# Stationary-weight projection of q and k with pieces placed by transfers, and transposed row maxima placed from one copy

## The chip, the cores and the metric

The kernel runs on one core of one Trainium2 chip. The metric is the device time of one launch in microseconds (us). TensorE is written PE, its weight loads PEld, VectorE DVE, ScalarE ACT, GpSimd POOL; SP (SyncE) computes nothing here and issues the transfers (DMAs).

## The reference

Eight batch elements of 512 positions and 256 features go through a layer norm, sliding-window attention with 32 query heads on 8 key/value heads, and a gate: silu of a projection of the 8-bit rounded input.

```
xn = layernorm(x)
q = xn @ Wq + bq; k = xn @ Wk + bk; v = xn @ Wv + bv     # 32, 8, 8 heads of 64
q, k = interleaved_rope(q, cos, sin) * SCALE, interleaved_rope(k, cos, sin) * SCALE
#   first = even * cos - odd * sin;  second = odd * cos + even * sin
scores = q k^T, masked to |i - j| <= 128; one sink logit per head joins the softmax
s = (softmax(scores with sink) without sink @ v) @ Wo + bo
x = x + s * silu(fp8(xn) @ W.T + b)
```

Products are kept near full float32 by splitting an operand into a rounded high part and a low remainder (names ending in hi/high and lo/low) and multiplying the parts.

## The kernel before

The work is 64 steps, one for each batch element (8) and key/value head (8, with its group of 4 query heads), and each step has 4 tiles q of 128 positions. The engines run their own programs and meet through semaphores. The order within a tile is written out by hand; each step works on three stages at once: it projects tile q of step it+2, turns and takes row maxima of step it+1, and does scores, exponentials, the weighted sum and the output projection of step it (the weighted sum one tile late, the transposition of its result two, the output projection three). Loops (Fori) run over batch elements and pairs of groups; two steps before the first are written apart and fill the pipeline while x is normalised and the weights are split.

In a tile, `project` (L974) multiplies the tile of x (stationary) with 384 columns of weights: 4 query heads, one key head and one value head. `projected` (DVE, L760) adds the bias; `turn` (POOL, L431 to L438) applies the rotation; `split_hi` (ACT) and `split_lo` (POOL, L444) make the parts side by side in `qk_parts`. TensorE then transposes them against an identity: `turn_q_full` (L983) each tile, `turn_k` (L995) once a step, and ACT copies the results (L534, L538). `score_rows` (L1016) gives scores by rows for the maxima (`maximum`, DVE L772), `negated` makes `neg_parts`, `turn_max` (L1001) transposes them, and ACT places the rows by 4 copies with a mask (L552) into partitions 64 to 71 of `qT_high`. So `scores` (L1028 and L1030, two matmuls for each block of 128 keys) gives scores with the maximum already taken off, `exps` (ACT L529) exponentiates them, `cut` (POOL L464) clears the corners, `weigh` (L1042) sums values, `turn_o` (L1051) transposes, and `out_project` (L1063) accumulates over the groups. The chunks `turn_x`, `turn_xq` and `ffn` stand in some tiles of steps 1, 6 and 7 of a batch element.

The wait that decides the order at a score is

```
at(pe, s_exp_done, NB, c + 1, blk - 1)
```

that is, with two score banks, a third block waits for the exponential of the first. In a tile of before, the projection and the turns stand between the second and the third block.

## Time and profile before

| | |
|---|---|
| time, median of 3 runs | 1935.78 us (1932.91 to 1942.27) |
| the profiled execution | span 1928.5 us from its first to its last instruction; the profile gives no device time of its own beside it |
| PE busy | 1818.4 us (94%) |
| DVE, ACT, POOL busy | 71%, 73%, 61% |
| mean granted TensorE clock | 0.983 |
| transfers | 20672 packets in SP's queue, 25.45 MB, 4.0% of 16 engines |

Times are us from the start of the span. In a line of a timeline the first number is the start and the second the duration; x6 means six instructions merged. In a group of the page the numbers after the bar are the busy time in us, the mean of one in ns, and the idle time of the engine just before them. In a line of windows stand the stretch, its length, the busy time of PE, PEld, DVE, ACT and POOL with the number of instructions, the granted clock of TensorE as a share of 2.4 GHz, the busy share of the DMA engines and GB/s. "issue" in the chain is time in which an engine waited for nothing that the profile shows.

### The profile page before, as it was taken

The numbers are of one execution on the slowest core, as the hardware profiler recorded it, in microseconds if no ns is written. First come the engines' busy times: TensorE is split into PE (matmuls) and PEld (weight loads), VectorE is DVE, ScalarE is ACT, GpSimd is POOL, SyncE is SP. The second block draws the span as 40 slices with busy tenths as digits, with TensorE's granted clock in tenths as the row PEclk, the third lists the DMA queues.
The fourth block names the chain that finished last, engine by engine and source line by source line (L and its number), as shares of the span: only waits on it lengthen the run. The fifth ranks groups of instructions, "written<-read, shape, count | busy, mean of one in ns | idle before, by whom it ended". The sixth has DMA issues, their size and how long they took to land.

```text
span 1928.5 us, 48655 instructions
## 1 busy us (share of the span) xinstructions
PE 1818.4 (94%) x13199; PEld 1707.6 (89%) x13199; DVE 1373.2 (71%) x4883; ACT 1406.3 (73%) x3764; POOL 1183.6 (61%) x1511
## 2 busy tenths in 40 slices
PE   3499999999999999999999999999999999999997
PEld 2399998999989999899989999899998999889996
DVE  8776776777767777767767777577777676776775
ACT  3277777777767777777867777677877787777775
POOL 4465656666566666666656666566666665665654
PEclk9699999999999999999999999899999999999999
DMA  5200000000000000000000000000000000000000
GB/s 191 82 8 2 0 1 25 12 2 0 13 20 5 1 0 18 19 2 0 1 19 18 2 0 1 30 7 2 0 18 19 2 1 1 18 24 2 0 1 17
DMA packets 20889, 28.07 MB, mean 15 GB/s; under 512 B 1344, under 2 KB 19264, under 8 KB 20544
## 3 DMA queue, kind: packets, MB, share of 16 engines
q1 hardware_dynamic: 20672, 25.45, 4.0%
q8 instruction: 103, 1.69, 0.4%
q14 instruction: 114, 0.93, 0.2%
HBM read 21.25 MB, written 4.19 MB: 13 GB/s over the span
## 4 chain that ended last, share of the span: by engine, by line
PE 86%; DVE 5%; issue 4%; ACT 1%; DMA 0%; DVEq 0%; POOLq 0%; POOL 0%; ACTq 0%
PE pv_bank L1042 26%; PE ring L974 15%; PE ring L1016 10%; PE acc L1063 9%; PE score L1028 8%; PE score L1030 7%; PE ring L983 5%; PE ring L1051 3%; PE ring L995 2%; PE ring L964 1%; PE ring L1001 1%; DVE junk L772 1%; DVE neg_max L781 1%; DVE sink_arg L786 1%; DVE proj L760 1%
## 5 line engine op out<-in xcount | busy, mean ns | idle before, releaser
L1042 PEld LDWEIGHTS pv_bank<-v,stage 128*128 128x128 f32 x5136 | 682.5, 192 | 4.7 <-issue 1.1
L1042 PE MATMUL pv_bank<-v,stage 128*128 128x65 f32 x5136 | 674.0, 266 | 0.9 <-DVE o_norm L800 0.9
L772 DVE CUSTOM_DVE_ANT_0 junk<-ring,mask 128x384 bf16<-128x384 f32 (+1 forms) x1036 | 507.0, 490 | 224.9 <-PE ring L1016 198.3
L529 ACT ACTIVATE stage<-score 128x512 f32<-128x512 f32 x640 | 357.0, 588 | 283.1 <-PE score L1030 282.3
L464 POOL TENSOR_SCALAR_AFFINE_SELECT stage<-stage 128x512 f32<-128x512 f32 x384 | 243.2, 641 | 425.1 <-ACT stage L529 425.1
L1016 PE MATMUL ring<-kT_high,qT_full 128*128 128x384 f32 (+1 forms) x1036 | 398.9, 385 | 16.6 <-DVE proj L760 15.4
L444 POOL TENSOR_TENSOR qk_parts<-turned,qk_parts 128x320 fp32r<-128x320 f32 x263 | 227.3, 864 | 207.0 <-ACT qk_parts L564 207.0
L552 ACT ACTIVATE qT_high<-ring,own_rows 8x128 fp32r<-8x128 f32 x1032 | 284.9, 345 | 13.7 <-PE ring L1001 7.3
L1028 PE MATMUL score<-qT_full,kT_high 128*128 128x512 f32 x640 | 267.7, 418 | 16.1 <-issue 14.9
L760 DVE TENSOR_TENSOR proj<-ring,bias 128x384 f32<-128x384 f32 x264 | 145.7, 552 | 183.7 <-PE ring L974 183.2
L1030 PE MATMUL score<-qT_high,kT_low 72*128 72x512 f32 x640 | 256.3, 400 | 0.0
L1016 PEld LDWEIGHTS ring<-kT_high,qT_full 128*128 128x128 f32 x1036 | 199.8, 193 | 50.3 <-DVE proj L760 15.8
L438 POOL TENSOR_TENSOR turned<-turned,turn_s 128x320 f32<-128x320 f32 x264 | 229.6, 870 | 20.7
L431 POOL TENSOR_TENSOR turned<-proj,cos 128x320 f32<-128x320 f32 x264 | 228.8, 867 | 21.9 <-DVE proj L760 21.9
L434 POOL TENSOR_TENSOR turn_s<-proj,sin 128x320 f32<-128x320 f32 x264 | 229.8, 870 | 0.0
L974 PE MATMUL ring<-w_hi,xT_hi 128*128 128x384 f32 (+1 forms) x528 | 197.0, 373 | 27.3 <-DVE proj L760 17.5
L534 ACT ACTIVATE qT_full<-ring 128x512 fp32r<-128x512 f32 x259 | 155.6, 601 | 43.3 <-PE ring L983 43.1
L974 PE MATMUL ring<-w_hi,xT_lo 128*128 128x384 f32 (+1 forms) x528 | 182.5, 346 | 0.0
L974 PE MATMUL ring<-w_lo,xT_hi 128*128 128x384 f32 (+1 forms) x528 | 182.0, 345 | 0.0
L983 PEld LDWEIGHTS ring<-ident_r,qk_parts 128*128 128x128 f32 x1036 | 156.4, 194 | 21.5 <-DVE inv_scale L821 0.3
L538 ACT ACTIVATE qT_high<-qT_full 64x512 fp32r<-64x512 f32 x259 | 163.3, 631 | 6.4
L1063 PE MATMUL acc<-wo_hi,oT_hi 128*128 128x256 f32 (+1 forms) x518 | 156.6, 302 | 0.4 <-DVE oT_lo L806 0.4
(110 smaller groups left out, 3282.4 us busy)
## 6 DMA issues: line engine op xcount, KB each, us to landing
x_in<-in_x SPq DMA_DIRECT2D x13, 512.0 KB, 3.6
x_res<-in_x SPq DMA_DIRECT2D x18, 256.0 KB, 3.3
out<-x_res SPq DMA_DIRECT2D x16, 256.0 KB, 2.2
stage<-in_w_qkv SPq DMA_DIRECT2D x4, 768.0 KB, 5.0
gate<-in_x SPq DMA_DIRECT2D x4, 512.0 KB, 4.1
stage<-in_w_o SPq DMA_DIRECT2D x4, 512.0 KB, 3.6
bias<-in_b_qkv SPq DMA_DIRECT2D x1, 1152.0 KB, 6.6
bias<-in_b_qkv SPq DMA_DIRECT2D x1, 384.0 KB, 7.8
```

What stands on the lines that cost most here:

```text
L434: nc.gpsimd.tensor_tensor(turn_s[:, :].rearrange("p (h i t) -> p h i t", i=D // 2, t=2), x_qk.rearrange("p (h i t) -> p h i t", i=D // 2, ...
L464: nc.gpsimd.affine_select(out=pr, in_=pr, compare_op=ALU.is_ge, fill=0.0, base=0, pattern=[[0, GROUP], [sign, P]], channel_multiplier=-sign) \
L529: nc.scalar.activation(prob[:, q % 2 * 3 + n, :], score[(FIRST[q] + n) % 2][:, :], ACT.Exp) \
L552: last = nc.scalar.activation(qT_high[D:D + NR, q, h * P:(h + 1) * P], ring[2][0:NR, 0:P], ACT.Copy, scale=own_rows[:, h:h + 1])
L772: nc.vector.tensor_tensor_reduce(junk[:, h % 2, 0:cols], ring[h % 2][:, 0:cols], mask[:, m0:m0 + cols], 1.0, LOWEST, ALU.add, ALU.max, row ...
L974: last = nc.tensor.matmul(ring[1][:, 0:PW], left[:, k, q * P:(q + 1) * P], of_group(right[:, k, :], g, PW), start=(n == 0), stop=(n == len ...
L983: last = nc.tensor.matmul(ring[0][:, h * P:(h + 1) * P], qk_parts[:, par, q, h * HW:h * HW + 2 * D], ident_r[:, :], start=True, stop=True)
L1016: nc.tensor.matmul(ring[h % 2][:, 0:cols], qT_full[:, q, h * P:(h + 1) * P], kT_high[:, par, k0 * P:k0 * P + cols], start=True, stop=True) ...
L1028: nc.tensor.matmul(score[blk % 2][:, :], kT_high[:, par, k * P:(k + 1) * P], qT_full[:, q, :], start=True, stop=False)
L1030: nc.tensor.matmul(score[blk % 2][:, :], kT_low[0:D + NR, par, k * P:(k + 1) * P], qT_high[0:D + NR, q, :], start=False, stop=True).then_i ...
L1042: last = nc.tensor.matmul(pv[:, h, :], prob[:, q % 2 * 3 + n, h * P:(h + 1) * P], v[:, par, k, :], start=(n == 0), stop=(n == len(BLOCKS[q ...
L1063: last = nc.tensor.matmul(acc[q // 2][:, (q % 2) * M:(q % 2 + 1) * M], left[:, q % 2, k * P:(k + 1) * P], w_g, start=fresh and k == 0 and ...
```

## The change

The weights become the stationary operand for q and k. The even and the odd elements of the four query heads of a group are 128 columns each, so `project` (now 128 weight columns against all 512 positions, six matmuls) gives them transposed already: `queries(a, 0)` and `queries(a, 1)` at the start of each step, for step a = it+2. Keys come for four groups at once (`QUAD`), twice a batch element, and values for all eight groups by tile, four times a batch element; `chunk_at` puts these into the tiles (1, 2), (1, 3), (5, 2), (5, 3) for keys and (7, 1), (7, 2), (7, 3) and (0, 1) of the next for values, as (group, tile). Bias and copy of q are on ACT (`even_out`, `odd_out`), the rotation and the low parts on POOL (`turn_even` to `second_low`), bias and rotation of k on DVE (`keys_turn`).

A group's pieces then lie 32 partitions to a head, and the scores need 64 in a row for each head, with a high part below. SP places them by transfers from SBUF to SBUF of 32 partitions by 512 elements (64 KB): `queries_in` twice, 12 transfers each, and `keys_in`, 6 transfers, every step. The row maxima are turned for two tiles at once, copied once by ACT, and placed by `rows_in`, 4 transfers of 2 partitions, twice a step. All loops are written out (no Fori), the normalised x stays in its input buffer, 8 instead of 9 elements are normalised ahead, and the first 8-bit rounding moves into step 0.

```diff
-            def turn(a, q):
...
-                    .broadcast_to([P, GROUP + 1, D // 2, 2])
-                nc.gpsimd.tensor_tensor(turned[:, slot, :].rearrange("p (h d) -> p h d", d=D),
-                                        x_qk.rearrange("p (h d) -> p h d", d=D), cos_q, ALU.mult) \
-                    .then_inc(s_turn_self, 1)
-                nc.gpsimd.tensor_tensor(turn_s[:, :].rearrange("p (h i t) -> p h i t", i=D // 2, t=2),
-                                        x_qk.rearrange("p (h i t) -> p h i t", i=D // 2, t=2)[:, :, :, ::-1],
-                                        sin_q, ALU.mult).then_inc(s_turn_self, 1)
-                at(pool, s_turn_self, 2 * TILES, a, 2 * q + 2)
-                nc.gpsimd.tensor_tensor(turned[:, slot, :], turned[:, slot, :], turn_s[:, :], ALU.add) \
-                    .then_inc(s_turned_done, 1)
-
-            def split_lo(a, q, par):
-                at(pool, s_hi_done, 2 * TILES, a, 2 * q + 2)
-                parts = qk_parts[:, par, q, 0:(GROUP + 1) * HW].rearrange("p (h w) -> p h w", w=HW)
-                nc.gpsimd.tensor_tensor(parts[:, :, 0:D], turned[:, q % 2, :].rearrange("p (h d) -> p h d", d=D),
...
+            def turn_even(a):
+
+                pool.wait_ge(s_even_done, a + 1)
+                upto(pool, s_qT_first_in, Q_IN * a)
+                upto(pool, s_qT_second_in, Q_IN * a)
+                nc.gpsimd.tensor_tensor(q_first[:, :], q_even[:, :], cos[:, :], ALU.mult).then_inc(s_rope, 1)
+                nc.gpsimd.tensor_tensor(q_second[:, :], q_even[:, :], sin[:, :], ALU.mult).then_inc(s_rope, 1)
+
+            def turn_odd(a):
+
+                pool.wait_ge(s_odd_done, a + 1)
+                nc.gpsimd.tensor_tensor(q_second_hi[:, :], q_odd[:, :], sin[:, :], ALU.mult).then_inc(s_rope, 1)
+                pool.wait_ge(s_rope, 6 * a + 3)
+                nc.gpsimd.tensor_tensor(q_first[:, :], q_first[:, :], q_second_hi[:, :], ALU.subtract) \
+                    .then_inc(s_rope, 1)
+
+            def turn_rest(a):
+
+                nc.gpsimd.tensor_tensor(q_odd[:, :], q_odd[:, :], cos[:, :], ALU.mult).then_inc(s_rope, 1)
+                pool.wait_ge(s_rope, 6 * a + 5)
+                nc.gpsimd.tensor_tensor(q_second[:, :], q_second[:, :], q_odd[:, :], ALU.add).then_inc(s_rope, 1)
+
+            def first_low(a):
+                pool.wait_ge(s_first_hi, a + 1)
+                nc.gpsimd.tensor_tensor(q_first[:, :], q_first[:, :], q_first_hi[:, :], ALU.subtract) \
+                    .then_inc(s_first_lo, 1)
+
+            def second_low(a):
+                pool.wait_ge(s_second_hi, a + 1)
+                nc.gpsimd.tensor_tensor(q_second[:, :], q_second[:, :], q_second_hi[:, :], ALU.subtract) \
+                    .then_inc(s_second_lo, 1)
...
+            def keys_in(t):
+
+                quad, r = t // QUAD, slice(t % QUAD * HALF, (t % QUAD + 1) * HALF)
+                sp.wait_ge(s_k_lo, 2 * quad + 2)
+                upto(sp, s_score_pe, NB * (t - 2))
+                upto(sp, s_kT_in, K_IN * t)
+                for row, part in ((0, k_first_hi), (HALF, k_second_hi), (D, k_first_hi), (D + HALF, k_second_hi)):
+                    sp.dma_start(kT_high[row:row + HALF, t % 3, :].bitcast(F32), part[r, :]).then_inc(s_kT_in, 16)
+                for row, part in ((0, k_first), (HALF, k_second)):
+                    sp.dma_start(kT_low[row:row + HALF, t % 3, :].bitcast(F32), part[r, :]).then_inc(s_kT_in, 16)
+
+            def queries_in(a, row, low, high, ready, done):
+
+                sp.wait_ge(ready, a + 1)
+                upto(sp, s_score_pe, NB * (a - 1))
+                upto(sp, done, Q_IN * a)
+                for h in range(GROUP):
+                    r = slice(h * HALF, (h + 1) * HALF)
+                    sp.dma_start(qT_full[row:row + HALF, a % 2, h, :].bitcast(F32), low[r, :]).then_inc(done, 16)
+                    sp.dma_start(qT_full[D + row:D + row + HALF, a % 2, h, :].bitcast(F32), high[r, :]) \
+                        .then_inc(done, 16)
+                    sp.dma_start(qT_high[row:row + HALF, a % 2, h, :].bitcast(F32), high[r, :]).then_inc(done, 16)
+
+            def rows_in(s, pair):
+
+                sp.wait_ge(s_max_rows_done, 2 * s + pair + 1)
+                if s == 0 and pair == 0:
+                    sp.wait_ge(s_ones_ready, 3)
+                for h in range(GROUP):
+                    sp.dma_start(qT_high[D + 2 * h:D + 2 * h + 2, s % 2, h, pair * 2 * P:(pair + 1) * 2 * P]
+                                 .bitcast(F32), turned_rows[2 * h:2 * h + 2, :]).then_inc(s_rows_in, 16)
+
+            def result(n, j):
+
+                sp.wait_ge(s_fin_done, n * 2 + j + 1)
+                sp.dma_start(out_t[n][:, 2 * j:2 * j + 2, :], x_res[:, 2 * j:2 * j + 2, :]).then_inc(s_out_put, 16)
+
+            def step(it):
+                n, k = it // KV, it % KV
+                t, a = it + 2, it + 2
+                if real(t) and t % QUAD:
+                    keys_in(t)
+                if real(it):
+                    rows_in(it, 1)
+                if k == 0 and n >= 1:
+                    result(n - 1, 0)
+                if real(it + 1):
+                    rows_in(it + 1, 0)
+                if real(t) and t % QUAD == 0:
+                    keys_in(t)
+                if real(a):
+                    queries_in(a, 0, q_first, q_first_hi, s_first_lo, s_qT_first_in)
+                    queries_in(a, HALF, q_second, q_second_hi, s_second_lo, s_qT_second_in)
+                if k == 0 and n >= 1:
+                    result(n - 1, 1)
...
+            def even_out(a):
+                act.wait_ge(s_q_pe, 2 * a + 1)
+                upto(act, s_rope, 6 * (a - 1) + 2)
+                nc.scalar.activation(q_even[:, :], ring[1][:, :], ACT.Identity,
+                                     bias=q_bias[:, a % KV * 2:a % KV * 2 + 1]).then_inc(s_even_done, 1)
...
+            def max_rows(s, pair):
+
+                act.wait_ge(s_max_turned_pe, 2 * s + pair + 1)
+                upto(act, s_rows_in, 16 * GROUP * (2 * s + pair))
+                nc.scalar.activation(turned_rows[:, :].bitcast(F32R), ring[2][0:NR, 0:2 * P], ACT.Copy) \
+                    .then_inc(s_max_rows_done, 1)
...
+            def project(col, done):
+
+                products = [(w, xs, k) for k in range(KT)
+                            for w, xs in ((w_hi, xT_hi), (w_lo, xT_hi), (w_hi, xT_lo))]
+                for n, (w, xs, k) in enumerate(products):
+                    last = nc.tensor.matmul(ring[1][:, :], w[:, k, col:col + P], xs[:, k, :], start=(n == 0),
                                             stop=(n == len(products) - 1))
-                last.then_inc(s_proj_pe, 1)
-
...
+            def queries(a, odd):
+
+                if odd:
+                    pe.wait_ge(s_even_done, a + 1)
+                else:
+                    upto(pe, s_max_done, TILES * GROUP * (a - 1) if a > 1 else 0)
+                    if a == KV * 0:
+                        pe.wait_ge(s_k_turned, 4)
+                    if a == 1:
+                        pe.wait_ge(s_odd_done, 1)
+                    if a == 2:
+                        pe.wait_ge(s_w_lo_done, N_CHUNKS)
+                project(W_Q + (a % KV * 2 + odd) * P, s_q_pe)
+
+            def turn_max(s, pair):
+                pe.wait_ge(s_neg_done, 2 * s + pair + 1)
+                upto(pe, s_max_rows_done, 2 * s + pair)
+                for t in range(2):
+                    last = nc.tensor.matmul(ring[2][0:NR, t * P:(t + 1) * P], neg_parts[:, pair, t, :], ident_r[:, :],
+                                            start=True, stop=True)
+                last.then_inc(s_max_turned_pe, 1)
+
+            def score_rows(b, q, h, it):
+
+                if q == 0 and h == 0:
+                    pe.wait_ge(s_qT_first_in, Q_IN * (b + 1))
+                    pe.wait_ge(s_qT_second_in, Q_IN * (b + 1))
+                    pe.wait_ge(s_kT_in, K_IN * (b + 1))
+                if h == 1:
+                    other = chunk_at(it // KV, it % KV, q)
+                    if q == 0 and real(it + 2):
+                        pe.wait_ge(s_odd_done, it + 3)
+                    elif other is not None:
+                        ring1_read(other)
+                upto(pe, s_max_done, TILES * GROUP * b + GROUP * q + h - 1)
+                k0, cols = window(q)
+                nc.tensor.matmul(ring[h % 2][:, 0:cols], qT_full[:, b % 2, h, q * P:(q + 1) * P],
+                                 kT_high[:, b % 3, k0 * P:k0 * P + cols], start=True, stop=True).then_inc(s_max_pe, 1)
```

**PE, start of a tile.** Before, tile 0 of a step: from the second pair of score matmuls over the transposition of the query parts (`L983`) to the projection (`L974`).

```order
L1028 MATMUL score<-qT_full,kT_high 128x512 [waits exp_done]
L1030 MATMUL score<-qT_high,kT_low 128x512
L91 REGISTER_ALU
L91 ISA [waits lo_done]
L983 MATMUL ring<-ident_r,qk_parts 128x128 [waits max_done]
L983 MATMUL ring<-ident_r,qk_parts 128x128 x3
L91 ISA
L974 MATMUL ring<-w_hi,xT_hi 128x384 [waits max_done]
L974 MATMUL ring<-w_lo,xT_hi 128x384
L974 MATMUL ring<-w_hi,xT_lo 128x384
L974 MATMUL ring<-w_hi,xT_hi 128x384
L974 MATMUL ring<-w_lo,xT_hi 128x384
```

The same place now, from the first pair of score matmuls to the first row of scores for the maxima (`L1086`); `L1107` and `L1109` are the score pairs, `L1037` the projection of the odd elements of the queries.

```order
L1107 MATMUL score<-qT_full,kT_high 128x512 [waits exp_done,rows_in]
L1109 MATMUL score<-qT_high,kT_low 128x512
L1107 MATMUL score<-qT_full,kT_high 128x512 [waits exp_done]
L1109 MATMUL score<-qT_high,kT_low 128x512
L1037 MATMUL ring<-xT_hi,w_hi 128x512 [waits even_done]
L1037 MATMUL ring<-xT_hi,w_lo 128x512
L1037 MATMUL ring<-xT_lo,w_hi 128x512
L1037 MATMUL ring<-xT_hi,w_hi 128x512
L1037 MATMUL ring<-xT_hi,w_lo 128x512
L1037 MATMUL ring<-xT_lo,w_hi 128x512
L1086 MATMUL ring<-kT_high,qT_full 128x256 [waits kT_in,max_done,qT_second_in,qT_first_in]
L1123 MATMUL pv_bank<-v,stage 128x65 [waits cut_done,norm_done,exp_done,v_done]
```

The transpositions are gone, the projection has become six wide matmuls (six more, for the even elements, stand ahead of these rows), and the first row of scores now waits for the transfers (`qT_first_in`, `qT_second_in`, `kT_in`).

**SP, one step.** Before, the loop over batch elements, which holds four transfers for results in eight steps:

```order
L356 DMA x_res<-in_x 128x2x256
L357 ISA
L359 DMA out<-x_res 128x2x256 [waits fin_done]
L360 ISA
L356 ISA [waits out_put]
L356 DMA x_res<-in_x 128x2x256
L357 REGISTER_ALU
L359 DMA out<-x_res 128x2x256 [waits fin_done]
```

Now a part of one step: the last two transfers of `keys_in`, the two calls of `rows_in`, and the beginning of `queries_in`.

```order
L365 DMA kT_low<-k_first 32x512
L365 DMA kT_low<-k_second 32x512
L385 DMA qT_high<-turned_rows 2x256 [waits max_rows_done]
L385 DMA qT_high<-turned_rows 2x256 x3
L385 DMA qT_high<-turned_rows 2x256 [waits max_rows_done]
L385 DMA qT_high<-turned_rows 2x256 x3
L374 DMA qT_full<-q_first 32x512 [waits qT_first_in,score_pe,first_lo]
L375 DMA qT_full<-q_first_hi 32x512
L377 DMA qT_high<-q_first_hi 32x512
L374 DMA qT_full<-q_first 32x512
L375 DMA qT_full<-q_first_hi 32x512
L377 DMA qT_high<-q_first_hi 32x512
```

Each step has 38 such transfers in one queue; the first of a `queries_in` waits for the low part, for all score matmuls of step it (`score_pe`), whose buffer it overwrites, and the other 11 follow without a wait.

## Rows read from the trace of the kernel before

**Rows 1.** The page, part 4: the chain that ended last, by engine.

```profile
PE 86%; DVE 5%; issue 4%; ACT 1%; DMA 0%; DVEq 0%; POOLq 0%; POOL 0%; ACTq 0%
```

**Rows 2.** Windows of one batch element and of one plain step.

```profile
756.26:981.56 225.30, 220.24 (x1634) 207.92 (x1633) 161.51 (x587) 171.97 (x464) 142.44 (x181) 1.00 0.03 8
842.41:869.25 26.84, 26.84 (x203) 25.61 (x202) 19.31 (x72) 20.88 (x57) 17.28 (x23) 1.00 0.01 2
```

**Rows 3.** Timeline of TensorE in plain steps, start and duration in us.

```profile
902.14 0.56 PE L983 MATMUL ring<-ident_r,qk_parts 128*128 128x128 f32 x4
902.54 0.39 PE L974 MATMUL ring<-w_hi,xT_hi 128*128 x1
...
903.63 0.40 PE L1028 MATMUL score<-qT_full,kT_high 128*128 128x512 f32 x1
...
904.39 0.78 PE L1042 MATMUL pv_bank<-v,stage 128*128 128x65 f32 x6
904.98 0.42 PE L1016 MATMUL ring<-kT_high,qT_full 128*128 128x384 f32 x1
...
907.68 0.36 PE L1063 MATMUL acc<-wo_hi,oT_hi 128*128 x1
...
908.47 0.40 PE L1028 MATMUL score<-qT_full,kT_high 128*128 128x512 f32 x1
...
909.42 0.56 PE L983 MATMUL ring<-ident_r,qk_parts 128*128 128x128 f32 x4
...
919.47 0.36 PE L1016 MATMUL ring<-kT_high,qT_full 128*128 128x256 f32 x1
919.67 0.38 PE L1051 MATMUL ring<-ident,o_norm 128*128 128x128 f32 x2
919.89 0.56 PE L1042 MATMUL pv_bank<-v,stage 128*128 128x65 f32 x4
```

**Rows 4.** Groups by line and shape on ScalarE and GpSimd.

```profile
L529 ACT ACTIVATE stage<-score 128x512 f32<-128x512 f32 x640 | 357.0, 588 | 283.1 <-PE score L1030 282.3
L464 POOL TENSOR_SCALAR_AFFINE_SELECT stage<-stage 128x512 f32<-128x512 f32 x384 | 243.2, 641 | 425.1 <-ACT stage L529 425.1
L451 POOL TENSOR_TENSOR x_res<-x_res,gate 128x512 f32<-128x512 f32 x18 | 22.9, 1272 | 20.4 <-DVE gate L753 15.2 <-DMA x_res<-in_x 5.2
```

**Rows 5.** Timeline of the queue engine SP: its DMA issues.

```profile
19.95 0.33 SPq L333 DMA_DIRECT2D stage<-in_w_ffn  x1
20.32 0.43 SPq L328 DMA_DIRECT2D x_in<-in_x  x1
...
65.14 0.37 SPq L328 DMA_DIRECT2D x_in<-in_x  x1
65.55 0.51 SPq L350 DMA_DIRECT2D bias<-in_b_qkv  x1
```

**Rows 6.** The page, part 6: one issue group, KB each, median us to landing.

```profile
out<-x_res SPq DMA_DIRECT2D x16, 256.0 KB, 2.2
```

**Rows 7.** The chain in order of time: two of its seven long "issue" pieces.

```profile
321.27 1.98 issue
...
546.61 2.39 issue
```

**Rows 8.** Windows of 8 us after waits of TensorE, clock column in view.

```profile
96.00:104.00 8.00, 8.00 (x45) 7.49 (x46) 3.28 (x13) 4.77 (x13) 3.86 (x5) 0.73 0.07 24
544.00:552.00 8.00, 5.61 (x36) 5.10 (x35) 3.37 (x14) 3.23 (x8) 2.53 (x4) 0.93 0.03 9
552.00:560.00 8.00, 8.00 (x43) 7.76 (x42) 4.58 (x19) 3.54 (x11) 3.97 (x5) 0.64 0.00 0
1232.00:1240.00 8.00, 8.00 (x36) 7.80 (x35) 2.46 (x9) 4.28 (x12) 4.04 (x5) 0.50 0.00 1
```

**Rows 9.** Timeline of TensorE: the first scores, and the last weighted sum.

```profile
95.95 0.79 PE L1028 MATMUL score<-qT_full,kT_high 128*128 128x512 f32 x1 [1.19 <-ACT xqT L513]
...
1913.02 1.97 PE L1042 MATMUL pv_bank<-v,stage 128*128 128x65 f32 x16 [0.88 <-DVE o_norm L800]
```

More of the change, by code:

```diff
@@ L889, in step @@
[L889 to L896 removed]
+                        if real(b):
+                            maximum(b, q, h)
@@ L928, in _ @@
[L928 to L934 removed]
+            dve.wait_ge(s_x_odd_got, 16)
+            statistics(gate, range(TILES))
+            moments_of(1)
+            keys_turn(0, 0)
+            keys_turn(0, 1)
+            normalise(1, gate, range(TILES))
+            measure(1)
```

1214 lines of the change are left out of this document (558 added, 656 removed).

## Prediction

> **What bounds the kernel now.** The chain that ended last comes first: 86% of the span is TensorE's work [rows 1], so TensorE's time per step is the time. The windows come next: a plain step (842.41 to 869.25) takes 26.84 us with PE busy throughout, a batch element of eight steps 225.30 us at full clock [rows 2]. Eight plain steps are 214.7; the other 10.6 us are `turn_x`, `turn_xq`, `ffn` and one idle piece of about 2 us at a loop head, which comes back under the clock. The timeline then gives prices by distance from start to start, since matmuls overlap: six of the projection 902.54 to 903.63, 1.09 us; four of `L983` .40; two score pairs 908.47 to 909.42, .95, so .237 for a matmul of 512 columns; six of `weigh` .59; six of `out_project` .79; a row of 256 columns .20, `turn_o` .22 [rows 3]. The other engines have slack; a score block costs ACT 588 ns, and a float32 operation of 128x512 costs POOL 1272 ns [rows 4].
>
> **What TensorE saves.** Removed from a step: 4 times 1.09 of projection, 4 times .40 of `turn_q_full`, and the eight of `turn_k`, which I put at .75 (four like `L983`, four only 64 wide): 6.7. Left are 20.1 us. Added: 12 matmuls for the queries, 2.85; for keys 12 in four steps, .71; for values 24 in eight, .71 (four `turn_max` stay four). That is 24.4. Of the 10.6 us a batch element the loop piece of 2.0 goes with the loops, leaving 1.1 a step. A new wait appears: in tiles 1 and 2 the third score block has nothing ahead of it. Two pairs take .95, but the bank is free only after .47 + .59 of ACT and some .2 of hand-over: .35 lost, twice a step, less where a chunk stands between; I take .5. TensorE alone would need 26.0 a step where it needs 28.2.
>
> POOL does not stop it: eight operations of 1.27, 1.3 for keys and six `cut` of .64 make 15.3 us a step, counted from when the buffers come free; its last low part is ready after 8 times 1.27 and five cuts, 13.4 us. DVE loses `projected` and half of `negated`, ACT 16 small copies and five large ones; both were under 75%.
>
> **What SP adds.** This term decides. Follow the cycle from R, where TensorE takes the first row of tile 0 in step it. In step it, `queries_in` may start only when all scores of the step are done, the first half of tile 3 (`score_pe`), because it overwrites the buffer that they read. Then 24 transfers go out one behind the other, and the first row of step it+1 waits for the last to land. TensorE works meanwhile on what lies outside the cycle: the rest of tile 3 (rows .8, `weigh` 4 times .59, turn and output 1.0), then 2.85 of queries and .95 of scores: 8.0, with chunks in tile 3 .6 more on average, 8.6. Inside lie 26.0 - 8.6 = 17.4 us.
>
> An issue: SP's rows show .33 and .37 where nothing precedes, with a gap of .04, and .43 and .51 where the transfer follows directly on another [rows 5]. So the pitch lies between .37 and .55. These had 128 partitions, the new ones 32; I take .43, nearer the short end. 23 pitches are 9.9. Landing: 256 KB from SBUF took 2.2 us [rows 6]; a quarter of that I put at 1.9. With .2 for the two waits the queue part is 12.0. The step becomes 17.4 + 12.0 = 29.4, and TensorE stands idle for 12.0 - 8.6 = 3.4 us, 4.0 in a plain step, at one place. Behind that row queue `weigh` and both `turn_max`; POOL's `turn_even` waits for the same landing, and behind it its `cut`, which is needed five us later. `keys_in` (6) and `rows_in` (8) go out before or after the 24, where SP has time.
>
> **The clock.** Seven waits of about 2 us stand in the chain at loop heads, as pieces "issue", 1.98 to 2.39 [rows 7]. After the one at 546.61 the granted clock fell from its high level, 2.4 GHz, to the low one, 1.2: .93 and then .64 in windows of 8 us, 3.4 us lost by (1 - clock) times 8. From 1232 to 1240 it was .50 throughout, 4.0 us lost in that window alone; after the wait for which scores begin at 96, .73, 2.2 us [rows 8]. Not every such wait costs something: the batch element from 756.26 holds one and has 1.00 [rows 2]. A wait of 3.4 to 4 us in every step is longer than any of these, so I expect a fall in nearly every step; I take 2.4 us, near the lowest, since packed work follows. The Trainium skill ("TensorE: Matmul & The Clock Gate", section "HAM oscillation — how this bites in real kernels") describes this pattern, matmul groups parted by waits for transfers that restart at the low clock each time. It speaks against the change: by it every step pays, by the rows of waits of 2 us only some, and the sum would be 29.4 without the fall and 31.8 with it. The rows are of shorter waits, so the lengths, not the page, carry my choice.
>
> **Sum.** Before, scores began at 96 us, and 15.5 us remained from the last weighted sum [rows 9]. I put the new fill at 88 (one element fewer to normalise and no rounding ahead, about 15, against some 7 that x loads now queue behind 30 transfers), the end at 16 again. The last two steps have no queries to fetch and the last no rows: 23 + 17.5. So 88 + 62 times 31.8 + 40.5 + 16 = 2116 us of span. The profiled span was 1928.5, the median of runs 1935.8; with these 7 more, about 2120.
>
> **Rivals.**
> - *TensorE keeps the path; faster.* If the queue part takes under 8.6 us, SP is hidden. With landing and waits at 2.1 this needs a pitch below .28, or a landing much shorter; no row shows so little, but none shows 32 partitions out of SBUF. Then 144.5 + 62 times 26.0 + 7 = about 1765, up to 1830. For it speaks that .33 is itself an issue to another place.
> - *Queue-bound, but the clock holds.* At .37, the isolated pitch, the queue part is 10.6, the step 28.0, the idle 2.0 us, as long as waits of which some cost nothing: 1890. With a fall in every second step 1965. It crosses the time of before at about 28.7 us a step.
> - *The transfers themselves are slow.* If SP's pitch is .52, as where one followed another at once, the step is 33.9 and the time 2255; if each of the 64 KB transfers takes .6 us because 32 partitions share few ways in, 35.7 and 2365. Against it: in two of the windows the DMA share is .00 and in none above .07 [rows 8], so nothing else is in the way.
>
> The Trainium skill ("SBUF — State Buffer", the section on DMA port swizzle) gives 189 GB/s for 32 partitions at 1 MiB. By an estimate from that page 64 KB take .35 us, less than an issue, so by it SP and not the ways into SBUF sets the pace; no run here shows it.
>
> **How the numbers follow.** Queue-bound with the clock falling .55 (2000 to 2250 by pitches of .38 to .52), TensorE-bound .13, queue-bound with clock mostly held .20, transfers slower still .12. About 0.5% is what a measurement of this kernel can tell from no change. Faster takes the second case and most of the lower part of the third: .26. Same .04. Slower .70. The range leaves out most of the fast case and half of the slowest: 1840 to 2290. With cases on both sides, the likeliest one's own range is 2000 to 2250.
>
> **What would show it.** In the new profile: PE idle before `L1086` for 3 to 4 us in each of 62 steps, put down to a transfer into `qT_full` or `qT_high`; SP issues of .37 to .50 from start to start, 24 in a row; the chain with SP or DMA above 25% of the span and PE near 60%; a mean granted clock under .95; PE busy share down to about 80%; small waits of .35 us at `L1107` in tiles 1 and 2; 128x512 operations on POOL at 1.27. Wrong would be: `L1086` without a wait (then the pitch or the landing was mis-sized and the first rival holds), a clock of .98 or more with the wait in place (then the second), or a landing of over 3 us while SP is done (the third). If POOL's `L497` comes later than the scores of tile 3, the rotation is the gate and not the queue.

## The result and the profile after

The changed kernel takes 2535.86 us (median of 4 runs, 2534.69 to 2544.95), the kernel before 1937.19 in the same comparison (1932.91 to 1942.27): a ratio of 1.313, 95% interval 1.308 to 1.319. It is slower, as forecast and by the mechanism forecast, but the time lies far outside the range of 1840 to 2290. The page of the changed kernel, its spans, busy times and chain, answers to [rows 1], where PE had 86%:

```profile
span 2533.0 us, 35309 instructions
PE 1891.3 (75%) x11139; PEld 1675.2 (66%) x11139; DVE 1187.7 (47%) x4157; ACT 720.9 (28%) x1509; POOL 1008.5 (40%) x1019
...
q1 hardware_dynamic: 113296, 149.84, 22.8%
...
PE 52%; issue 19%; SPq 12%; DVE 3%; ACT 3%; POOL 3%; DMA 3%; POOLq 0%; DVEq 0%
```

No engine is over 75%: a cycle of waits sets the time, not an amount of work. Its waits (engine, line, releaser: total us, times, longest):

```profile
POOL q_first L473 <- DMA qT_high<-q_second_hi: 958.5, 62, 23.5
...
PE ring L1086 <- issue: 508.2, 63, 13.8
```

TensorE stands 8 us in each step before the first row of tile 0. SP's timeline of one step (start, duration), which answers to [rows 5], begins with the 24 transfers:

```profile
1202.39 0.54 SPq L374 DMA_DIRECT2D qT_full<-q_first  x1
1202.97 0.59 SPq L375 DMA_DIRECT2D qT_full<-q_first_hi  x1
1203.61 0.58 SPq L377 DMA_DIRECT2D qT_high<-q_first_hi  x1
1204.23 0.59 SPq L374 DMA_DIRECT2D qT_full<-q_first  x1
...
1216.26 0.59 SPq L375 DMA_DIRECT2D qT_full<-q_second_hi  x1
1216.90 0.59 SPq L377 DMA_DIRECT2D qT_high<-q_second_hi  x1
...
1241.77 0.54 SPq L374 DMA_DIRECT2D qT_full<-q_first  x1
```

TensorE's timeline has the row that waits for them:

```profile
1218.96 0.55 PE L1086 MATMUL ring<-kT_high,qT_full 128*128 128x256 f32 x1 [8.35 <-issue]
```

From these rows the cycle can be taken apart: 24 issues from 1202.39 to 1217.49 (15.1 us, .63 from start to start), 1.5 from the end of the last issue to the row, 22.8 until the next queries may start: 39.4 us. Read in the same way over the 62 steps, the mean is 15.4 + 1.5 + 21.1 = 38.0 us. In 47 of them the next queries start .07 us after the last score matmul. In the other 15, every fourth step, `keys_in` stands directly ahead of the queries, and SP is still issuing keys: it starts the queries 2.9 to 5.0 us after the scores, 50.1 us in all. The longest of these, where the last score ends at 214.45:

```profile
214.05 0.40 PE L1109 MATMUL score<-qT_high,kT_low 72*128 72x512 f32 x1
```

```profile
218.79 0.59 SPq L365 DMA_DIRECT2D kT_low<-k_second  x1
219.49 0.52 SPq L374 DMA_DIRECT2D qT_full<-q_first  x1
```

The clock, in windows of the step from 1202.39 (the number behind the busy times is the granted clock):

```profile
1210.00:1214.00 4.00, 0.61 (x3) 0.18 (x1) 0.00 (x0) 0.69 (x1) 0.00 (x0) 1.00 0.43 109
1214.00:1218.96 4.96, 0.00 (x0) 0.03 (x1) 0.00 (x0) 0.00 (x0) 0.00 (x0) 0.57 0.41 103
1218.96:1223.00 4.04, 4.04 (x20) 4.04 (x21) 0.96 (x5) 0.47 (x2) 3.96 (x4) 0.50 0.36 89
1223.00:1227.00 4.00, 4.00 (x17) 3.51 (x17) 2.73 (x9) 0.98 (x2) 1.63 (x2) 0.50 0.01 4
1227.00:1231.00 4.00, 3.63 (x24) 3.40 (x22) 2.07 (x5) 2.28 (x4) 3.56 (x4) 0.83 0.01 2
1231.00:1235.00 4.00, 4.00 (x27) 3.62 (x27) 3.39 (x15) 2.23 (x5) 2.08 (x3) 1.00 0.00 0
```

The clock falls to its low level, 1.2 GHz, inside the wait, and the next 8 us and more of packed work run at that level.

### The profile page after: what moved, and what is told of

Its sections match the earlier page's. It is cut to its first block, busy times and chain, and to the rows that moved or that the text cites. A ratio compares the mean times of both kernels' runs of the same rounds, so it can differ in the third digit from the quotient of the medians.

```text
span 2533.0 us, 35309 instructions
## 1 busy us (share of the span) xinstructions
PE 1891.3 (75%) x11139; PEld 1675.2 (66%) x11139; DVE 1187.7 (47%) x4157; ACT 720.9 (28%) x1509; POOL 1008.5 (40%) x1019
## 3 DMA queue, kind: packets, MB, share of 16 engines
q1 hardware_dynamic: 113296, 149.84, 22.8%
## 4 chain that ended last, share of the span: by engine, by line
PE 52%; issue 19%; SPq 12%; DVE 3%; ACT 3%; POOL 3%; DMA 3%; POOLq 0%; DVEq 0%
PE pv_bank L1123 18%; PE ring L1086 8%; PE acc L1146 7%; PE score L1107 5%; PE ring L1037 5%; PE score L1109 4%; SPq L375 4%; SPq L374 4%; DMA qT_high<-q_first_hi 3%; SPq L377 3%; PE ring L1133 2%; ACT stage L611 2%; PE ring L1046 2%; SPq L363 1%; POOL q_second L497 1%
## 5 line engine op out<-in xcount | busy, mean ns | idle before, releaser
L1086 PE MATMUL ring<-kT_high,qT_full 128*128 128x384 f32 (+1 forms) x1024 | 435.2, 426 | 574.3 <-issue 508.2
L1086 PEld LDWEIGHTS ring<-kT_high,qT_full 128*128 128x128 f32 x1024 | 229.9, 225 | 620.0 <-issue 555.3
L1107 PE MATMUL score<-qT_full,kT_high 128*128 128x512 f32 x640 | 283.0, 442 | 13.3 <-ACT stage L611 13.1
L1109 PE MATMUL score<-qT_high,kT_low 72*128 72x512 f32 x640 | 271.0, 423 | 0.0
L1107 PEld LDWEIGHTS score<-qT_full,kT_high 128*128 128x128 f32 x640 | 136.0, 213 | 66.3 <-ACT stage L611 48.4
L1037 PE MATMUL ring<-xT_hi,w_hi 128*128 128x512 f32 x320 | 145.8, 456 | 27.2 <-ACT q_even L617 18.9
L1146 PE MATMUL acc<-wo_hi,oT_hi 128*128 128x256 f32 x512 | 162.3, 317 | 0.6 <-DVE oT_lo L885 0.6
L1146 PE MATMUL acc<-wo_lo,oT_hi 128*128 128x256 f32 x512 | 161.5, 316 | 0.0
L1146 PE MATMUL acc<-wo_hi,oT_lo 128*128 128x256 f32 x512 | 160.8, 314 | 0.0
L1109 PEld LDWEIGHTS score<-qT_high,kT_low 72*128 72x128 f32 x640 | 134.4, 210 | 17.9
L1037 PE MATMUL ring<-xT_hi,w_lo 128*128 128x512 f32 x320 | 131.9, 412 | 0.0
L1037 PE MATMUL ring<-xT_lo,w_hi 128*128 128x512 f32 x320 | 131.4, 411 | 0.0
L885 DVE TENSOR_TENSOR oT_lo<-ring,oT_hi 128x256 fp32r<-128x256 f32 x256 | 108.6, 424 | 34.6 <-ACT oT_hi L652 31.5
L1146 PEld LDWEIGHTS acc<-wo_hi,oT_hi 128*128 128x128 f32 x512 | 116.4, 227 | 0.8 <-DVE oT_lo L885 0.8
```

The lines of the kernel that those rows point to most:

```text
L885: nc.vector.tensor_tensor(oT_lo[:, q % 2, :], ring[2][:, 0:KT * P], oT_hi[:, q % 2, :].bitcast(F32), ALU.subtract).then_inc(s_oT_lo_done, 1)
L1037: last = nc.tensor.matmul(ring[1][:, :], w[:, k, col:col + P], xs[:, k, :], start=(n == 0), stop=(n == len(products) - 1))
L1086: nc.tensor.matmul(ring[h % 2][:, 0:cols], qT_full[:, b % 2, h, q * P:(q + 1) * P], kT_high[:, b % 3, k0 * P:k0 * P + cols], start=True, s ...
L1107: nc.tensor.matmul(score[blk % 2][:, :], kT_high[:, c % 3, k * P:(k + 1) * P], qT_full[:, c % 2, :, q * P:(q + 1) * P], start=True, stop=F ...
L1109: nc.tensor.matmul(score[blk % 2][:, :], kT_low[0:D + NR, c % 3, k * P:(k + 1) * P], qT_high[0:D + NR, c % 2, :, q * P:(q + 1) * P], start ...
L1146: last = nc.tensor.matmul(acc[q // 2][:, (q % 2) * M:(q % 2 + 1) * M], left[:, q % 2, k * P:(k + 1) * P], right[:, col:col + M], start=fre ...
```

## The experiments

**Theory**: SP's issues and what lands behind them set the step, and the clock adds to it. Rivals: the bytes set it; a wait on another engine does; it is the other half of the change, the maxima. Times not given with an interval are of one run; the kernel before stood at 1926 to 1938 beside all of them.

**16 transfers in place of 24.**

```
-    sp.dma_start(qT_high[row:row + HALF, a % 2, h, :]..., high[r, :]).then_inc(done, 16)
-Q_IN = 16 * 3 * GROUP
+Q_IN = 16 * 2 * GROUP
```

> The changed kernel without the 8 transfers of a step that copy the high parts of the queries into qT_high; rows 0 to 63 of qT_high stay zero, so the correction of the scores by the keys' low parts is left out. 16 transfers stand in the cycle instead of 24. The changed kernel issues at .634 us from start to start and has steps of 39.4 us. Count theory (SP's issues, one behind the other, set the step): 8 x .634 = 5.1 us less a step, step 34.3, some 2210 us in all, pitch still .63. If the clock also recovers with the shorter wait, up to 2 us more: 2090. Rival, the landing or some other wait sets the step: under 2 us less, over 2400.

Measured 2177.9 us, clock .882. The mean step is 10.3 + 1.8 + 20.3 = 32.4: 5.6 us less, 5.1 in the issues and .8 in the inside part, with .3 more behind the last issue. The number of transfers counts.

**Half the bytes.**

```
-    ...dma_start(qT_full[row:row + HALF, a % 2, h, :]..., low[r, :])
+    ...dma_start(qT_full[row:row + HALF, a % 2, h, 0:256]..., low[r, 0:256])
```

> The changed kernel with the same 24 transfers a step for the queries, each of columns 0 to 255 instead of 0 to 511, so half the bytes; the queries of tiles 2 and 3 stay zero, so the scores of these tiles are not the reference's. If the pitch of .634 us is the cost of issuing: unchanged, .60 to .64, landing .1 to .3 us less, time within 1% of 2536. If the bytes set it (32 partitions share few ways in, or the engines' queues back up): pitch .32 to .45, step 33 to 35, time 2130 to 2250.

Measured 2538.8 us. SP's timeline:

```profile
1217.40 0.59 SPq L375 DMA_DIRECT2D qT_full<-q_first_hi  x1
1218.03 0.59 SPq L377 DMA_DIRECT2D qT_high<-q_first_hi  x1
1218.67 0.59 SPq L374 DMA_DIRECT2D qT_full<-q_first  x1
```

The pitch is .63 again, though the busy share of the DMA engines falls from .41 (1204.39 to 1212.39 in the changed kernel) to .18 (1214.46 to 1222.46 here). With 64 KB each, issuing sets the pace and the bytes do not.

**TensorE's wait filled.**

```
+    if q == 0 and real(b) and real(it):
+        pe.wait_ge(s_max_done, TILES * GROUP * b + GROUP * q)
+        for i in range(30):
+            nc.tensor.matmul(ring[0][:, :], w_hi[:, 0, 0:P], xT_hi[:, 0, :], start=True, stop=True)
     row(0)
```

> The changed kernel with 30 more matmuls of 512 columns a step (their result is overwritten) ahead of the first row of tile 0, where TensorE stands waiting for the transfers; at full clock they are some 7 us, the wait is 8.4. Nothing else differs. If the granted clock (.83 in the mean) costs time inside the cycle, as the difference of 22.8 us measured and 17.4 worked out from first row to next transfers says: work is added and the kernel gets faster, first row to next transfers 17.5 to 20, step 34 to 36.5, 2200 to 2350 us, clock above .93. Rival, the 22.8 us were other waits: clock up, but the time the same within 1%, or slower.

Measured 2486.2 us, clock .927: 1890 matmuls more and 50 us less, where I had expected 186 at least. Windows from the first row to the next transfers, three steps:

```profile
1202.65:1221.34 18.69, 17.95 (x127) 16.53 (x128) 14.27 (x47) 7.88 (x19) 13.09 (x13) 1.00 0.08 21
...
1275.66:1297.38 21.72, 21.72 (x125) 20.22 (x126) 12.71 (x46) 7.10 (x17) 13.14 (x13) 0.81 0.07 17
...
1349.92:1367.93 18.01, 17.88 (x127) 16.61 (x128) 12.71 (x49) 7.01 (x17) 14.23 (x15) 1.00 0.12 33
```

The steps differ in work, so each is compared with the same step of the changed kernel, from the first row to the end of the last score. In 21 of the 62 steps the filled kernel is at clock 1.00 and the changed kernel is not: 17.2 us for 20.1. So a fall of the clock costs 2.9 us. In three steps the changed kernel holds 1.00 itself, and takes 16.3 to 16.9 us for 16.1 filled. Over all steps the filled kernel won 1.5 us in the inside part, and lost .7 again: the 30 matmuls outlast some of the waits, and in most steps the clock fell anyway.

**A transfer by itself.** At the end of the changed kernel, bursts of eight (or six) with nothing else running:

```
+    for b_, h_ in spots:
+        sp.dma_start(qT_full[0:HALF, b_, h_, :].bitcast(F32), q_first[0:HALF, :]).then_inc(s_probe, 16)
+    sp.wait_ge(s_probe, 16 * 8)
...
+        sp.dma_start(qT_full[0:2, b_, h_, 0:2 * P].bitcast(F32), q_first[0:2, 0:2 * P])...
...
+    for i_ in range(6):
+        sp.dma_start(stage[:, i_ * 512:(i_ + 1) * 512], w_ffn[:, :]).then_inc(s_probe, 16)
```

> The changed kernel, and at its end bursts of 8 transfers one behind the other with nothing else running, from SP: 32x512 within SBUF (from low partitions and from partition 64 up), 128x512, 128x128, 32x128, 2x256, then 6 from DRAM of 128x512 and 6 of 32x512, then 8 of 32x512 from ACT. The bursts overwrite nothing that is still read. If issuing costs a fixed amount for a transfer within SBUF: .58 to .63 for each shape, 128x128 and 2x256 too. If it grows with what is moved or with the partitions: 2x256 under .4 and 128x512 over .63. Before showed .33 to .51 for transfers of 128 partitions from DRAM: I expect .35 to .5 for those. ACT: the same pitch as SP, so that two queues would halve the time. Whole time: 2536 plus some 60 us.

SP's timeline, in which a burst is one row with the sum of its time; L448 is 32x512, L454 128x512, L463 2x256, all within SBUF; L466 and L469 come from DRAM, 128x512 and 32x512. The last row is ACT's own burst of 32x512:

```profile
2549.05 4.96 SPq L448 DMA_DIRECT2D qT_full<-q_first  x8
...
2561.86 5.10 SPq L454 DMA_DIRECT2D qT_full<-q_first  x8
2568.77 4.97 SPq L457 DMA_DIRECT2D qT_full<-q_first  x8
...
2581.31 4.89 SPq L463 DMA_DIRECT2D qT_full<-q_first  x8
2587.23 2.73 SPq L466 DMA_DIRECT2D stage<-in_w_ffn  x6
2594.36 2.66 SPq L469 DMA_DIRECT2D stage<-in_w_ffn  x6
```

```profile
2598.71 5.09 ACTq L736 DMA_DIRECT2D qT_full<-q_first  x8
```

Divided by the count, within SBUF a transfer costs .61 to .64 us to issue whatever its shape, 2 KB or 256 KB; from DRAM .44 to .46. Here the prediction's rows misled: [rows 5] holds no transfer with both ends in SBUF.

**One transfer for four pieces.** The weights' columns (and the rows of cos and sin) are put in another order, so that the pieces of four heads lie in one row of 128 partitions:

```
-wq = ...transpose(0, 1, 2, 5, 3, 4)
+wq = ...transpose(0, 1, 2, 5, 4, 3)
-    for h in range(GROUP): ...
+    for dst, part in ((qT_full[row:row + HALF, a % 2, :, :], low), ...):
+        sp.dma_start(dst.bitcast(F32), part[:, :]).then_inc(done, 16)
```

> The changed kernel with the columns of the query and key weights put in another order (piece row ahead of head, the tables of cos and sin to match), so that the four head pieces of one part lie as 128 partitions in a row and one transfer of 256 KB places all four: 6 transfers a step where there were 24. The probe showed 128x512 within SBUF at the same pitch as 32x512. Count theory: the queue part is 5 x .63 + .5 + a landing of 1.5 to 2.2 = 5.2 to 5.9 us, less than the 8.6 that TensorE works outside the cycle, so that the wait at the first row goes away, the clock holds above .97, and TensorE sets the step: 26.0 by the prediction's sum, 27.4 if the inside part is 18.8 as the filled kernel showed at full clock. Time 1765 to 1860 us, faster than the kernel before (1936). Rival, the work that was moved to transfers was never what the time went to and something else of the change costs (POOL, the rows of maxima): over 1936.

Measured 2361.0 us, ratio 1.223 [1.219, 1.228]. This expectation fell. The issues take 3.9 us, but the landings do not follow (the last number is the median from issue to landing):

```profile
qT_full<-q_first SPq DMA_DIRECT2D x64, 256.0 KB, 4.2
qT_full<-q_first_hi SPq DMA_DIRECT2D x64, 256.0 KB, 5.6
qT_high<-q_first_hi SPq DMA_DIRECT2D x64, 256.0 KB, 6.9
qT_full<-q_second SPq DMA_DIRECT2D x64, 256.0 KB, 8.2
qT_full<-q_second_hi SPq DMA_DIRECT2D x64, 256.0 KB, 9.6
qT_high<-q_second_hi SPq DMA_DIRECT2D x64, 256.0 KB, 10.7
```

First and last issue are 3.25 us apart, so first and last landing are 3.25 + 10.7 - 4.2 = 9.75 apart: 1.95 us for each 256 KB (134 GB/s). In the mean the first row came 14.2 us after the first issue, for 16.9 in the changed kernel. 8.6 lie under TensorE's work; there the gain ends. Windows from 2 us after the first issue of a step, first here, then in the changed kernel (the last two numbers are the busy share of the 16 DMA engines and GB/s):

```profile
1123.86:1131.86 8.00, 6.18 (x35) 4.77 (x33) 3.27 (x13) 2.73 (x5) 0.00 (x0) 1.00 1.08 132
```

```profile
1204.39:1212.39 8.00, 6.22 (x35) 4.81 (x34) 3.27 (x13) 2.74 (x5) 0.00 (x0) 1.00 0.41 102
```

With merged pieces the share reads 1.08, so all 16 engines are busy throughout, and they move 132 GB/s where the changed kernel moves 102 at .41. 128x512 into 128 partitions went out every .64 us without falling behind (eight were sent and landed between 2561.86 and 2568.77, above: 304 GB/s at a busy share of .79). So where four pieces go into the same 32 partitions, the transfers themselves are a second limit close behind the issues. Why they keep the engines busy so long is not shown. The Trainium skill ("SBUF — State Buffer", the section on DMA port swizzle) gives 189 GB/s for 32 partitions at 1 MiB a transfer; these merged pieces stay under that figure.

**Two queues.** The 12 transfers of the second halves are issued from ACT at the end of its step:

```
-    queries_in(a, HALF, q_second, q_second_hi, s_second_lo, s_qT_second_in)      # SP
+    if q == 3 and real(a):
+        second_in(a)                                                             # ACT
```

> The changed kernel with the 12 transfers of the second halves issued from ACT at the end of the step and the 12 of the first halves from SP. If each engine issues at its own .634 us: both done after 7.6 us + landing 1.5 = 9.3; ACT's own work (even_out, which the odd projection waits for) is held back behind its 12 issues, so the first row comes at about 10 us instead of 17: step 29 to 31, 1950 to 2080 us, wait at the first row 1 to 3 us. Rival, the two queues share what limits the pitch (.634 for both together): no gain, over 2450.

Measured 2228.1 us, better than one queue but later than expected. Both queues issue their 12 side by side, in 8.0 (SP) and 8.3 us (ACT) in this step, and the wait at the first row is gone. But ACT's next work, `oT_hi`, stands behind its issues, DVE's `oT_lo` and `row_max` behind that, and TensorE's projection behind those: for 3.9 us in this step, 261.0 us in all where the changed kernel has 27.2.

```profile
1173.24 0.51 PE L1051 MATMUL ring<-xT_hi,w_hi 128*128 128x512 f32 x1 [3.94 <-DVE row_max L861]
```

**More bursts**, at the end of the merged kernel:

```
+    sp.dma_start(out_t[BATCH - 1][:, i_ % 4, :], x_res[:, i_ % 4, :])...     # 6, to DRAM
+    sp.dma_start(qT_full[0:HALF, b_, h_, :]..., q_first[0:HALF, :])...       # 8 from SP, 8 from ACT at once
+    nc.gpsimd.dma_start(qT_full[0:HALF, b_, h_, :]..., q_first[0:HALF, :])   # 8 from POOL
```

> The kernel with merged transfers, and at its end: SP issues 4 and 2 transfers of 128x256 from SBUF to DRAM (the last result again), then 2 merged ones of 256 KB, then 8 of 32x512 within SBUF at the same time as 8 from ACT, then 8 from POOL alone. If the source in SBUF is what makes .63 out of .45: .6 for SBUF to DRAM. If it is both ends in SBUF: .45. SP and ACT together: .63 each (queues independent) or about 1.2 each (shared). POOL: no row shows it; .6 to 1.2 us each. Merged transfer landing 2.2 us.

To DRAM an issue took .33 to .46 us: both ends in SBUF, not the source alone, make the .63. SP and ACT issue at once without slowing each other much:

```profile
2371.31 5.36 SPq L457 DMA_DIRECT2D qT_full<-q_first  x8
```

```profile
2371.28 5.09 ACTq L730 DMA_DIRECT2D qT_high<-q_first  x8
```

```profile
2378.71 4.14 POOL L591 DMA_DIRECT2D qT_full<-q_first  x8 [20.97 <-SPq L460]
```

That is 16 times 64 KB issued in some 5.4 us, 195 GB/s; all had landed 2.0 us later. POOL issues one in .52. The two merged transfers, with nothing else running, landed 4.2 and 5.2 us after their issue, not 2.2: they are slow by themselves.

**The merged kernel without the maxima's transfers.**

```
-    rows_in(it, 1)
-    rows_in(it + 1, 0)
```

> The kernel with merged transfers without the 8 transfers a step that place the row maxima (rows 64 to 71 of qT_high stay as they were set at the start, so the scores are not lessened by their maximum). Prices the other half of the change by itself. If SP has time for them, as the rows of the changed kernel say (they go out between two groups for the queries): same as merged within .5%. Rival, they lie in the way of the queries or scores wait for them: 1 us a step less, 60 us or more.

Measured 2366.6 us beside 2361.0. In this kernel the transfers of the maxima cost nothing; turning and copying the maxima is still in it and is not priced.

**Second queue on POOL**, all 24 transfers of 64 KB, the 12 of the second halves from POOL after its last `cut`, where it waits for the landing anyway:

```
+    if q == 3 and real(a):
+        second_in(a)              # nc.gpsimd.dma_start
```

> The changed kernel (24 transfers of 64 KB a step) with the 12 of the second halves issued by POOL at the end of its step, where it waits for the landing anyway, and 12 by SP. The probe gave POOL 8 issues in 4.1 us, .52 from start to start. Both are done after 7.6 us, landing 1.5: 9.1 us against the 8.6 that TensorE works outside the cycle, and nothing is held back on ACT as in the kernel with two queues. Step 27.5 to 28.5 with a wait of .5 to 1 us that the clock mostly survives: 1850 to 1930 us, faster than before. Rival: POOL's issues are slower beside work of DVE, or POOL itself comes late with the next low parts (it starts turn_even only after its 12 issues, but it waited for the landing before too): step over 30, over 2000 us.

Measured 2080.7 us, ratio 1.071 [1.060, 1.081]: 455 us of the loss of 600 come back, less than expected. In the mean of the 62 steps 9.0 us pass from the first issue of either queue to the last (SP's own 12 take 8.1), 2.4 from there to the first row (1.5 with one queue), and 19.5 to the next issue. With two queues the landing is later (2.0 for each with one):

```profile
qT_full<-q_second POOLq DMA_DIRECT2D x256, 64.0 KB, 2.7
...
qT_full<-q_first SPq DMA_DIRECT2D x256, 64.0 KB, 2.9
```

**Merged and two queues**, SP with ACT, then SP with POOL:

```
+    DMA(dst.bitcast(F32), part[:, :]).then_inc(s_qT_second_in, 16)   # 3 from act / nc.gpsimd
```

> The kernel with merged transfers (6 of 256 KB a step, each into 32 partitions, one landing 1.3 us after the other: 194 GB/s), the 3 into rows 0 to 31 and 64 to 95 from SP, the 3 into rows 32 to 63 and 96 to 127 from ACT. If the 1.3 us are a limit of the 32 partitions written, the two queues go side by side: done after 3 x 1.35 + 2.8 = 6.9 us, hidden behind 8.6: TensorE-bound, step about 27, clock above .95, 1800 to 1880 us, faster than before. If the 1.3 us are a limit of all 16 engines together or of the source: 14 us as before, no gain, 2300 to 2400.

> As the kernel before it, with POOL for ACT. Limit of the partitions written: 1790 to 1880 us; ACT holds no work back, so up to 20 us less than with ACT. Otherwise 2300 to 2400.

Measured 2289.1 (1.180 [1.175, 1.186]) and 2349.0 us (1.213 [1.207, 1.219]). Neither is hidden. The landings stay late (SP's third 11.3 us after its issue in the first of them). The expectations took the landings as 1.3 us apart, which is the step of the column without the .65 between the issues; it is 1.95. The DMA engines are as busy with two queues as with one (1.08 and 130 GB/s from 1091.22 to 1099.22 in the first of these kernels), so a second queue has nothing to fill, and the two halves' going to other rows does not help either.

**Only what the first row needs ahead of it.** SP issues the 8 of the first halves into `qT_full`, POOL the 8 of the second, and the 8 copies into `qT_high` follow on SP under a semaphore of their own, which the scores wait for later; then the same order from SP alone:

```
+    pe.wait_ge(s_high_in, 32 * GROUP * (c + 1))      # scores, tile 0
+    for row, high in ((HALF, q_second_hi), (0, q_first_hi)):
+        for h in range(GROUP):
+            sp.dma_start(qT_high[row:row + HALF, a % 2, h, :]...).then_inc(s_high_in, 16)
```

> The changed kernel with the same 24 transfers in another order and from two queues, output complete: SP issues the 8 of the first halves into qT_full, POOL at the end of its step the 8 of the second halves, and SP then the 8 copies into qT_high under a semaphore of their own. The first row of tile 0 waits for qT_full alone; the copies are waited for by the scores a quarter step later and by POOL before it writes over their source. 16 transfers of 64 KB from two queues: 7 x .634 + .6 + landing 1.5 to 2.9 = 6.5 to 8 us, under the 8.6 that TensorE works outside the cycle. So the wait goes away, clock above .97, step 26.0 (the prediction's sum for TensorE alone) to 27.5 (as the filled kernel's inside part says): 1780 to 1890 us, faster than before. Rival: another wait takes its place (POOL's turn_even late, the next low parts late): over 1936.

> The same order, all from SP: 16 into qT_full, then 8 into qT_high, waited for later. It parts two explanations of what 16 instead of 24 gave: if only the place of the first row's wait counts, this complete kernel is as fast as the one that left the 8 copies out (2178 us, step 32.6): 2170 to 2220. If SP's total of issues counts (the copies then hold back keys_in and rows_in, which others wait for): over 2250.

Measured 1986.5 us, ratio 1.032 [1.027, 1.038], over the range expected, and 2250.9. The wait at the first row is nearly gone: the rows' group stood idle for 574.3 us in the changed kernel and for 115.7 here, 33.4 of it for transfers. But another entry of SP's queue is now on the path. TensorE's groups of the first of these kernels (busy, mean ns, idle before and its releasers):

```profile
L1109 PE MATMUL ring<-kT_high,qT_full 128*128 128x384 f32 (+1 forms) x1024 | 401.3, 393 | 115.7 <-DMA qT_full<-q_first_hi 33.4 <-DVE row_max L870 19.3 <-DVE k_second_hi L849 16.7
...
L1132 PE MATMUL score<-qT_full,kT_high 128*128 128x512 f32 x640 | 275.8, 431 | 45.6 <-DMA qT_high<-turned_rows 30.2 <-ACT stage L634 15.1
```

With one queue the eight late copies cost 73 us against leaving them out (2178): SP's total counts too, though less than the place of the wait.

**The maxima ahead of the keys.**

```
+    if real(it): rows_in(it, 1)
     if real(t) and t % QUAD: keys_in(t)
-    if real(it): rows_in(it, 1)
```

> The kernel with 16 transfers from two queues ahead of the first row and the copies behind, with one exchange in SP's order: the second pair of row maxima (4 transfers) ahead of the keys of the step (6) instead of behind them. In the kernel without it TensorE's scores waited 30.2 us in all for qT_high<-turned_rows, and half a clock for 4 to 6 us behind some of these waits. If that is what is left of SP on the path: 30 us less for the waits and 10 to 25 for the clock, 1930 to 1950, the same as the kernel before within 1%. Rival: the keys come late in their place, and the first row waits for them: 1980 or more.

Measured 1937.1 us (12 runs; the traced one took 1957.7, the longest), ratio 1.003 [1.000, 1.006]: the wait fell from 30.2 to .9 us, and the loss is gone. A wait of the change's own is left in tiles 3 with keys:

```profile
1099.80 0.39 PE L1109 MATMUL ring<-kT_high,qT_full 128*128 128x256 f32 x1 [1.43 <-DVE k_second_hi L849]
```

**The second row later in those tiles.**

```
+    if other is not None and other[0] == "k" and q == 3:
+        weighed(1); weighed(2); row(1)
```

> The last kernel, with one exchange in TensorE's order: in the 16 tiles 3 that hold a projection of keys, two groups of weighted sums (1.2 us) stand ahead of the second row instead of behind it. There TensorE waits 1.4 us at that row for DVE, which reads the keys out of the same bank, and behind these waits the granted clock is .5 for some 6 us (two of the profile's windows of 4 us read so). Theory, a short wait costs little in itself and 3 us through the clock: 16 x (1.2 + 3) = 67 us less, 1870 to 1890, faster than before. Rival, the clock falls there for another reason or the wait moves to another row: 17 us less or none, 1920 to 1940.

Measured 1916.8 us (12 runs), ratio .992 [.989, .995]: faster than the kernel before, by .8%. By the two ratios the gain over the last kernel is 1.1%, some 21 us. The idle time before the rows fell by as much (124.1 to 103.1 us; 16.8 of it were the waits for `k_second_hi`, which are gone), so the theory that each wait cost 3 us more through the clock fell. In windows of the middle (700 to 1180) the clock reads .99 for .96, but the mean of all runs is .95 for both kernels; it falls elsewhere instead.

## Why the prediction was right and wrong

**Right**: the place and the kind of the bound. The cycle from the first row of tile 0 over the last scores, 24 issues and the landing back to the first row is what the trace shows in 47 of 62 steps, and in the other 15 with SP's keys in it; TensorE is idle at the row in nearly all, POOL's `turn_even` waits for the same landing, and the clock falls. Fewer issues ahead of that row gave time back every time (24: 2536; 16: 2178; 12 in SP's queue and 12 in POOL's: 2081; 8 in each: 1987).

**Wrong, the pitch**: "I take .43, nearer the short end". It is .63 in most steps and .64 in the mean, outside both ends of the bound (.37 to .55). The 23 pitches take 14.8 us a step where 9.9 were put: 4.9 x 62 = 304 us of the 417 missing from the span. The step that failed was to bound a transfer within SBUF by rows of transfers from or to DRAM. The bursts show that the kind of the ends matters and the shape does not; the argument over 128 or 32 partitions was about the wrong property. The rival with .6 us per transfer gave 2365 and had the right size for another reason than the one it was given: not the ways into SBUF, since half the bytes changed nothing. The Trainium skill's figure for 32 partitions ("SBUF — State Buffer", the section on DMA port swizzle) was used for the estimate that 64 KB take less than an issue; the run with half the bytes agrees, with .63 for either size. The likeliest case's own range was also mis-stated: by the same sum pitches of .38 to .52 give 2050 to 2255, not 2000 to 2250.

**Landing and waits**: right. 2.1 us were put from the last issue's start to the row, and 2.1 are measured.

**SP's own queue**: put at nothing. "`keys_in` (6) and `rows_in` (8) go out before or after the 24, where SP has time": in every fourth step SP has no time, and the keys hold back the queries (the rows from 214.05, above). With the .07 us of the other steps that is .9 us a step, 53 us.

**The clock**: 2.4 us were put in each step; 2.9 are measured where it fell, in 59 of 62 steps, so 2.8 in the mean, 25 us more. The mean granted clock of .83 looks worse than that; part of the time at the low level is the wait itself, as in the window from 1214.00.

**The inside part**: 17.4 us were summed at full clock. Measured are 20.2 to the last score, less 2.8 for the clock: 17.4. This is an estimate, since 2.8 comes from 21 steps. It holds waits that were not summed, and the third blocks wait less than was put: .22 us, in 60 places, for .35 twice a step. The four terms make 304 + 53 + 25 = 382 with nothing for the inside part; 62 x (38.0 - 31.8) is 384.

**The ends**: outside the 62 steps the span holds 2533 - 62 x 38.0 = 177 us where 144.5 were put. Scores begin at 117.7 and not at 88.

**Signs**: the wait at `L1086`, the low clock and 1.27 us on POOL came as said, but the wait is 8.0 us for 3 to 4, and SP and DMA hold 15% of the chain for over 25%.

**TensorE alone**: 26.0 us were summed. In the last kernel, where SP and the first row hardly matter, the shortest steps take 24.7 to 25.4 us, and the mean of the steps is 28.1, with waits of 1.9 us a step at rows and scores (103.1 and 16.9 us in all) and a clock of .95. The sum is about right; that TensorE would then run without waits is not. The first rival's 1765 us were reached by no kernel here; the nearest took 1916.8.

## What to carry to other kernels

Before a few large copies on an engine are traded for many small transfers, count the issues in the longest wait for them and price each by a transfer of the same two ends; here .63 us within SBUF against .33 to .46 to or from DRAM, for 2 KB as for 256 KB. Count what else stands in that queue, too: six issues for the keys held back every fourth step. Then ask which of them the first waiter needs: splitting the group by its waiters and over two queues, one of them an engine that waits at that place anyway, brought back 549 of 599 us, and two exchanges of order the rest and a little more. Merging pieces helps only as far as the transfers themselves keep up.

## What the runs showed of the hardware

Not expected: a transfer with both ends in SBUF costs SP .61 to .64 us to issue for 2x256 as for 128x512; SP and ACT issue side by side at that pitch, and POOL issues one in .49 to .52. Eight transfers of 256 KB into 128 partitions keep up with .64 us each, but pieces of 256 KB into 32 partitions land some 1.95 us apart, with all 16 DMA engines busy (1.08 where 64 KB pieces show .41), from one queue or from two. TensorE ran 8 us and more of packed work at its low clock after a wait of 8 us.
